# A vision tower on one core: scale folded into weights, small operations moved between engines, instruction lists in another order

## The chip, the cores and the metric

The kernel runs on one core of a Trainium2 chip. The time is the device time of one execution, in microseconds (us). The core has TensorE (matmuls, its weight loads shown as PEld), VectorE (DVE), ScalarE (ACT), GpSimd (POOL) and a queue engine (SP) that issues the DMAs. Each engine works off its own list of instructions in order; semaphores tie the lists together.

## The reference

The input x holds complex states, 64 time steps by 128 channels by 64 states by 2 (real, imaginary). The output is 64 x 129 x 1024. Per step (cut to what matters):

```python
h = s4d_kernel(log_dt, C=x, B, inv_A_real, A_imag, L=1024)      # (64, 128, 1024): sum over states of C * V**l
h = concatenate([broadcast(cls_tok), h], axis=1)                # (64, 129, 1024)
h = h + attn(layernorm(h))
h = h + ffn(layernorm(h))
# attn: down to 128, gelu, two hydra layers, gate, up to 1024
u = gelu(x @ w_down.T + b_down); xmid = u
u = hydra(hydra(u))
alpha = sigmoid(gate1)
out = x + (xmid + alpha * xmid + (1 - alpha) * u) @ w_up.T + b_up
# hydra: in-projection to z, xBC, dt; causal conv of 7 taps and silu; a forward and a backward
#   state-space scan over the 64 steps (4 heads of 64, 16 states); skip; times silu(z); rms norm; out-projection
# ffn: base linear 1024 -> 1024 + LoRA of 8 experts of rank 16, weighted by a router softmax over
#   15 logits of which the top 8 are kept
```

## The kernel before, in words

A tile is two of the 128 channels with their 64 steps each: 128 rows of 1024. There are 64 such tiles and one for the class token, 65 in all. The kernel is a software pipeline over iterations i = 0 to 69. In iteration i each engine works on up to five tiles at once: tile i (S4D kernel, first norm, down projection), tiles i-1 and i-2 (stages "H" and "G", the two halves of a hydra layer; the first layer of one tile and the second layer of the tile two behind it are done side by side), tile i-4 ("D": gate, up projection, second norm) and tile i-5 ("E": router, base linear, LoRA, store). All stages run in iterations 5 to 63. Iterations 8 to 61 are a hardware loop of two iterations per pass, the others are written out. On the way a tile's first norm result and u rest in DRAM (`carried`).

What each engine does in an iteration, and in which order, is an explicit list of calls at the end of its body: `grams()`, `turn_xs()`, ... for TensorE, `kernel_p()`, `gram(0)`, ... for VectorE, and so on. A step waits only for the semaphores named in it, and for what stands ahead of it in its engine's list. Large fp32 products are done as three fp32r matmuls with weights and activations split into a high and a low part (`w_hi`, `w_lo`, `XHI`, `XLO`); transposes and small products are plain fp32.

The steps that matter here:

- S4D (tile i): `turn_x` (TensorE) transposes the states into a PSUM bank; `keep_x` (ScalarE, L991) copies 256 columns to XTC, 128 real and 128 imaginary; `shift_real` (VectorE) and `shift_imag` (GpSimd) multiply them by three time shifts; `shift_none` (GpSimd, L831) copies the unshifted real part into W; `shift_sum` adds; `s4d(0)`, `s4d(1)` multiply; `keep_h` (ScalarE) copies the result to T; `stats_1` (VectorE), `root_1` (GpSimd), `shift_1` (VectorE, L1341: NM1 = -mean x root) and `norm_1` (ScalarE) make the normed H, which `turn_a` transposes and `down` projects. `deviation_1` and `carry_h` (GpSimd, L875) make h + norm(h) for the residual.
- Hydra: `grams`, `turn_xs`, `decay_sums` (TensorE), `gram`, `gram_forth`, `gram_sum`, `mix_matrix` (VectorE), `exp_decays` (ScalarE), `mix`, `skip` (GpSimd), `add_skip`, `times_z` (VectorE), `squares`, `norm_y` (ScalarE), `mean_square` (VectorE), `root_y` (GpSimd), `turn_y`, `keep_y`, `project_out`. `layer_out` (VectorE, L1282) copies the layer's output to U, the input of the next layer. `project_x`, `project_bc`, `project_z` project the next input; `conv` (VectorE, two halves by six taps) and `scale_bc` with `add_bc` (ScalarE and GpSimd, L895) convolve; `softplus(0..12)`, `split_decays`, `decays_forth`, `decays_back` make the decays for the next iteration; `silu_x`, `silu_bc` (L1066) end the convolution, and the next `grams` wait for them.
- Gate (tile i-4): `gated_a` (VectorE, L1348) scales xmid by 1 + alpha, `gated_b` (L1354) adds (1 - alpha) times the layer's output from PSUM; the sum is split (`gated_hi`, `gated_lo`) and multiplied in `up(0)`, `up(1)`. Then `residual`, `stats_2`, `root_2`, `shift_2` (VectorE, L1384), `norm_2`, `turn_d`, `split_hi`, `split_lo`.
- Router and FFN (tile i-5): `route(a, b)` and `bases(h, a, b)` are the blocks a to b-1 of 128 inputs of the router with LoRA-down (144 columns) and of half h of the base linear (512 columns), three matmuls per block. Router steps 0 to 8 (VectorE) with `exp_router`, `turn_h`, `keep_w` and `weighted_lo` (the split into HWS) lead to `lora(0)`, `lora(1)`, which close the banks; `final(0)`, `final(1)` add the residual, and SP stores.

The functions of one engine name lines that the profile shows under a helper: L929 is ScalarE's `copy`, L1512 the three matmuls of `ffn`.

Of the kernel before, what the change touches and what calls it, by code (L numbers as in the profile page):

```python
# [23 lines left out]
F32 = mybir.dt.float32  # L24
F32R = mybir.dt.float32r
I32 = mybir.dt.int32
ALU = mybir.AluOpType
# [3 lines left out]
P = 128  # L31
# [23 lines left out]
def build(nc, x, cls_tok, log_dt, tok_B, inv_A_real, A_imag, w_down, b_down, w_up, b_up, gate1, in_w,  # L55
# [19 lines left out]
    with ExitStack() as keep:  # L75
# [55 lines left out]
        with ExitStack() as tmp:  # L131
# [61 lines left out]
            s_albe, s_tab, s_vals, s_chain = tsem("s_albe"), tsem("s_tab"), tsem("s_vals"), tsem("s_chain")  # L193
            s_red, s_dec, s_sin, s_exp = tsem("s_red"), tsem("s_dec"), tsem("s_sin"), tsem("s_exp")
# [174 lines left out]
            def _(act):  # L369
# [87 lines left out]
            def _(dve):  # L457
# [115 lines left out]
                def second_parts(n):  # L573

                    for k, (src, m, dst, lo, _, _) in enumerate(jobs):
# [8 lines left out]
                        TT(lo, cols, dst.bitcast(F32), ALU.subtract).then_inc(s_lo, 1)  # L584

                for c in range(CHUNKS):
# [4 lines left out]
                    if c == 0:  # L591
# [5 lines left out]
                        link(TS(al1[:, :], al1[:, :], 1.0, None, ALU.add))  # L597
                second_parts(1000)
# [11 lines left out]
        XTC = sb("XTC", [P, 2, 2, CS])  # L610
# [60 lines left out]
        per = dict(cls_in=(1, 16), xswap=1, xt=1, xtc=1, wr=1, wi=2, wsum=1, v1=1, v2=1, vsum=1,  # L671
                   km=2, hev=4, st1=4, rs1=1, sd1=1, nm1=1, xh1=1, tt=1, tr1=2, xte=2, down=1, gelu=1,
                   pin=3, xms=1, conv0=4, conv=NCONV, cbm=TAPS - 1, cbc=TAPS - 1, dtc=NDT, asp=2, edt=1, xs=3, sz=1, trx=1, gram=1, xse=1,
# [61 lines left out]
        with nc.Block() as block:  # L735

            @block.sync
            def _(sp):
# [34 lines left out]
                def load_x(t, p):  # L773
                    wait(sp, t - 2, xt=1, xswap=1, v1=1, wr=1, v2=1, wi=2)
# [25 lines left out]
            def _(pool):  # L800
                def body(i, p):
# [21 lines left out]
                    def shift_imag():  # L823

                        if A:
                            wait(pool, i, xtc=1)
                            wait(pool, i - 1, wsum=1)
                            inc(pool.tensor_tensor(WI[:, :, :, :], XTC[:, 1, :, :].unsqueeze(2).broadcast_to([P, 2, 3, CS]),
                                                   TB[:, p, :, TSI].unsqueeze(3).broadcast_to([P, 2, 3, CS]), ALU.mult), "wi")

                    def shift_none():  # L831
                        if A:
                            wait(pool, i, xtc=1)
# [27 lines left out]
                    def root_1():  # L861
                        if A1:
                            wait(pool, i, st1=4)
                            wait(pool, i - 1, xh1=1, sd1=1)
                            inc(pool.tensor_tensor(RS1[:, :], VE1[:, :], half_neg[:, 0:1], ALU.pow), "rs1")  # L865

# [40 lines left out]
                    shift_none()  # L907
# [19 lines left out]
            def _(act):  # L927
# [3 lines left out]
                def body(i, p):  # L931
# [59 lines left out]
                    def keep_x():  # L991
                        if A:
                            wait(act, i, xt=1)
                            wait(act, i - 1, wr=1, wi=2)
                            copy(XTC[:, :, :, :].rearrange("p a b c -> p (a b c)"), bK[:, 0:256], "xtc")

# [33 lines left out]
                    def keep_y():  # L1030
                        if G:
                            wait(act, r, tyn=1, mm=1)
                            wait(act, r - 1, outp=1)
                            copy(YT[:, :, :].rearrange("p a b -> p (a b)"), bZ[:, :], "yte")

# [50 lines left out]
                    keep_x()  # L1086
                    keep_xs()
                    exp_decays()
# [8 lines left out]
                    keep_h(1, 0)  # L1097
                    keep_h(1, 1)
                    keep_y()
# [696 lines left out]
```

## Time and profile before

| | us |
|---|---|
| median of 3 runs | 2343.29 (2339.07 to 2344.38) |
| the profiled execution's own time | 2339.94 |
| its span, first to last instruction | 2338.2 |
| TensorE busy (weight loads) | 2161.3, 92% (1805.6, 77%) |
| VectorE busy | 1847.3, 79% |
| ScalarE busy | 1528.2, 65% |
| GpSimd busy | 1091.2, 47% |
| mean DMA rate | 57 GB/s |

The page cuts the span into 40 slices. TensorE is at 90% or more in the sixth and up to the last but one; its granted clock is in the top tenth from the sixth slice on. The first five slices or so are the set-up (weights transposed and split, tables) and the first iterations, in which few tiles are under way. Matmul durations are modelled and overlap, so it is the distance from start to start that counts. An engine's idle time on a line is followed by who ended it; "issue" means that nothing the profile shows was waited for.

### The profile page before, as it was taken

The numbers are of one execution on the slowest core, as the hardware profiler recorded it, in microseconds if no ns is written. First come the engines' busy times: TensorE is split into PE (matmuls) and PEld (weight loads), VectorE is DVE, ScalarE is ACT, GpSimd is POOL, SyncE is SP. The second block draws the span as 40 slices with busy tenths as digits, with TensorE's granted clock in tenths as the row PEclk, the third lists the DMA queues.
The fourth block names the chain that finished last, engine by engine and source line by source line (L and its number), as shares of the span: only waits on it lengthen the run. The fifth ranks groups of instructions, "written<-read, shape, count | busy, mean of one in ns | idle before, by whom it ended". The sixth has DMA issues, their size and how long they took to land.

```text
span 2338.2 us, 51899 instructions
## 1 busy us (share of the span) xinstructions
PE 2161.3 (92%) x14117; PEld 1805.6 (77%) x14117; DVE 1847.3 (79%) x4980; ACT 1528.2 (65%) x2921; POOL 1091.2 (47%) x1350
## 2 busy tenths in 40 slices
PE   1356799999999999999999999999999999999998
PEld 1245688888888888888888888888888888888776
DVE  6847688888888888888888888888888888888764
ACT  2546576766677766667666767666777666676652
POOL 2534355444455444455444554444554444554331
PEclk9756799999999999999999999999999999999999
DMA  4400122112222122221122221122211222211211
GB/s 92 117 29 24 35 64 64 42 54 63 63 63 61 35 61 63 63 63 48 47 63 63 63 63 40 55 63 63 63 58 36 63 63 63 63 47 47 69 39 33
DMA packets 90061, 132.61 MB, mean 57 GB/s; under 512 B 20379, under 2 KB 63559, under 8 KB 90006
## 3 DMA queue, kind: packets, MB, share of 16 engines
q1 hardware_dynamic: 79176, 125.60, 18.2%
q10 hardware_dynamic: 10830, 6.35, 1.1%
q8 instruction: 25, 0.41, 0.1%
q14 instruction: 30, 0.25, 0.0%
HBM read 55.17 MB, written 76.74 MB: 56 GB/s over the span
## 4 chain that ended last, share of the span: by engine, by line
issue 43%; PE 27%; POOL 9%; DVE 7%; ACT 6%; POOLq 1%; DVEq 0%; ACTq 0%; DMA 0%; SPq 0%
PE bank L1611 5%; PE bank L1512 5%; POOL CB L901 4%; PE bank L1567 3%; PE bank L1542 2%; DVE NF L1241 2%; ACT L1006 2%; POOL XD L852 2%; PE bank L1685 1%; PE bank L1669 1%; POOL RS L886 1%; PE bank L1544 1%; PE bank L1543 1%; POOL RS L865 1%; PE bank L1659 1%
## 5 line engine op out<-in xcount | busy, mean ns | idle before, releaser
L1512 PE MATMUL bank<-w_hi,XHI 128*128 128x512 f32 (+1 forms) x1560 | 622.9, 399 | 0.0
L1512 PE MATMUL bank<-w_lo,XHI 128*128 128x512 f32 (+1 forms) x1560 | 554.7, 356 | 0.0
L1512 PE MATMUL bank<-w_hi,XLO 128*128 128x512 f32 (+1 forms) x1560 | 554.4, 355 | 0.0
L1147 DVE SCALAR_TENSOR_TENSOR CX<-bank,cw,CX 128x252 f32<-128x252 f32 (+5 forms) x804 | 335.7, 460 | 61.8 <-ACT CX L944 61.6
L901 POOL TENSOR_TENSOR CB<-CB,CM 48x252 f32<-48x252 f32 (+5 forms) x402 | 292.7, 728 | 153.6 <-ACT CM L929 142.7
L1512 PEld LDWEIGHTS bank<-w_hi,XLO 128*128 128x128 f32 x1560 | 295.5, 189 | 46.9
L1512 PEld LDWEIGHTS bank<-w_lo,XHI 128*128 128x128 f32 x1560 | 296.8, 190 | 41.4
L1512 PEld LDWEIGHTS bank<-w_hi,XHI 128*128 128x128 f32 x1560 | 296.4, 190 | 41.2
L929 ACT ACTIVATE T<-bank 64x512 f32<-64x512 f32 x256 | 151.4, 592 | 261.1 <-PE bank L1601 256.5
L865 POOL TENSOR_TENSOR RS<-VE,half_neg 128x1 f32<-128x1 f32 x65 | 35.5, 546 | 369.9 <-DVE VE L1339 369.9
L892 POOL TENSOR_TENSOR RB<-m_gt,AS 128x512 fp32r<-128x512 f32 x134 | 164.9, 1231 | 56.8 <-DVE AS L1413 56.8
L929 ACT ACTIVATE CM<-CR,cwb 48x256 f32<-48x256 f32 x402 | 181.5, 497 | 3.7 <-POOL CB L901 1.5
L859 POOL TENSOR_TENSOR RS<-MS,half_neg 128x2 f32<-128x2 f32 x67 | 46.9, 700 | 242.8 <-DVE MS L1270 242.8
L1601 PE MATMUL bank<-VB,W 128*128 128x256 f32 x512 | 148.9, 415 | 7.4 <-DVE W L1212 5.2
L1395 DVE TENSOR_TENSOR XLO<-bank,XHI 128x512 fp32r<-128x512 f32 x130 | 89.9, 692 | 72.1 <-ACT XHI L929 72.1
L1401 DVE TENSOR_TENSOR RF<-m_lt,AS 128x512 fp32r<-128x512 f32 x134 | 142.9, 1105 | 0.0
L1611 PE MATMUL bank<-XHT,wdT 128*128 128x128 f32 x1040 | 135.8, 287 | 4.5 <-ACT XHT L929 4.5
L929 ACT ACTIVATE XHI<-bank 128x512 fp32r<-128x512 f32 x130 | 77.6, 597 | 94.7 <-PE bank L1567 94.7
L1611 PEld LDWEIGHTS bank<-XHT,wdT 128*128 128x128 f32 x1040 | 129.4, 203 | 6.1 <-ACT XHT L929 6.1
L844 POOL TENSOR_TENSOR NB<-GB,sp_dt 128x512 f32<-128x512 f32 x67 | 95.9, 1431 | 77.4 <-DVE GB L1224 77.4
L852 POOL TENSOR_TENSOR XD<-XS,DD 128x512 f32<-128x512 f32 x67 | 84.6, 1263 | 99.0 <-DVE DD L1232 54.2
L1601 PEld LDWEIGHTS bank<-VB,W 128*128 128x128 f32 x512 | 89.9, 196 | 23.1 <-issue 5.9
(295 smaller groups left out, 5332.5 us busy)
## 6 DMA issues: line engine op xcount, KB each, us to landing
carried<-T SPq DMA_DIRECT2D x65, 512.0 KB, 4.8
T<-carried SPq DMA_DIRECT2D x65, 512.0 KB, 3.9
out<-HB SPq DMA_DIRECT2D x129, 256.0 KB, 3.2
tables<-tab SPq DMA_DIRECT2D x8, 560.0 KB, 4.3
TB<-tables SPq DMA_DIRECT2D x64, 70.0 KB, 2.7
carried<-U SPq DMA_DIRECT2D x65, 64.0 KB, 3.6
XM<-carried SPq DMA_DIRECT2D x65, 64.0 KB, 4.8
XI<-in_x SPq DMA_DIRECT2D x128, 32.0 KB, 2.8
```

The source lines that it names most:

```text
L844: inc(pool.tensor_tensor(NB[:, :, :].rearrange("p (a h) t -> p a h t", a=2), GB[:, :, :].unsqueeze(2).broadcast_to([P, 2, NH, CS]), dtB, A ...
L852: inc(pool.tensor_tensor(XD[:, :, :], v3(XS[:, :], HD), DD[:, :].unsqueeze(2).broadcast_to([P, 2 * NH, HD]), ALU.mult), "xd")
L892: inc(pool.tensor_tensor(RB[:, part, :, :], m_gt[:, :].unsqueeze(1).broadcast_to([P, 2 * NH, CS]), decays(1, part), ALU.mult), "rb")
L901: inc(pool.tensor_tensor(CB[:, :, s:CS], CB[:, :, s:CS], CM[:, s % 3, :, 0:CS - s], ALU.add), "cbc")
L929: inc(act.activation(dst, src, ACT.Copy, scale=scale), name)
L1147: inc(STT(CX[:, c, :, s:CS], src[:, :, 0:CS - s], cw[:, c, k:k + 1], CX[:, c, :, s:CS], ALU.mult, ALU.add), "conv")
L1395: inc(TT(XLO[:, p, ks, :], v3(bT[:, :], P), XHI[:, p, ks, :].bitcast(F32), ALU.subtract), "xlo")
L1401: inc(TT(RF[:, part, :, :], m_lt[:, :].unsqueeze(1).broadcast_to([P, 2 * NH, CS]), decays(0, part), ALU.mult), "rf")
L1512: ins = mm(bank[:, 0:c1 - c0], xs_[:, 1 - p, k, :], ws[:, k, c0:c1], start=(c0 == HID and k == 0 and n == 0), stop=(last == k and n == 2))
L1567: ins = tr(bT[:, P * k:P * (k + 1)], T2[:, (4 * g + k) * P:(4 * g + k + 1) * P], ident[:, :])
L1601: ins = mm(bK[:, 256 * s:256 * (s + 1)], W[:, b, 2 * s:2 * s + 2, :].rearrange("p a c -> p (a c)"), VB[:, b, :, :].rearrange("p a c -> p ( ...
L1611: ins = mm(bK[:, 0:P], wdT[:, k, :], XHT[:, k, :], start=(k == 0), stop=(k == KC - 1))
```

## The change

- al1 = 1 + sigmoid(gate) is multiplied into the up projection's weights when they are transposed and split; be1 becomes (1 - alpha) / (1 + alpha). `gated_a` falls away, and GT = be1 x layer output + xmid.
- `shift_1` and `shift_2` go from VectorE to GpSimd, as a `tensor_scalar` of one column.
- `layer_out` goes from VectorE to ScalarE, where it also waits for `gated_b`, which reads the same bank.
- `keep_x` makes two copies of 128 columns: the real part goes into W's unshifted place, the imaginary part to XTC. `shift_none` falls away, and `shift_real` reads W.
- The lists of all four engines are put in another order.

The parts of the diff follow, in the order set-up, GpSimd, ScalarE; `shift_2` is `shift_1` with NM2, MV2, RS2.

```diff
-                        jobs.append((src, rows, hi, lo, 1.0, n))
+                        jobs.append((src, rows, hi, lo, al1[:, 0:1] if kind == "u" else 1.0, n))
...
+                    if n >= 0 and pieces[n][0] == "u":
+                        act.wait_ge(s_gate, 1)
...
-                        TT(lo, cols, dst.bitcast(F32), ALU.subtract).then_inc(s_lo, 1)
+                        if scale == 1.0:
+                            TT(lo, cols, dst.bitcast(F32), ALU.subtract).then_inc(s_lo, 1)
+                        else:
+                            STT(lo, cols, scale, dst.bitcast(F32), ALU.mult, ALU.subtract).then_inc(s_lo, 1)
...
+                        link(dve.reciprocal(gate[:, :], al1[:, :]))
+                        TT(be1[:, :], be1[:, :], gate[:, :], ALU.mult).then_inc(s_gate, 1)
...
-                    def shift_none():
-                        if A:
-                            wait(pool, i, xtc=1)
-                            wait(pool, i - 1, km=2)
-                            apart(pool)
-                            inc(pool.tensor_copy(W[:, :, 0, :], XTC[:, 0, :, :]), "wi")
+                    def shift_1():
+                        if A1:
+                            wait(pool, i, rs1=1)
+                            wait(pool, i - 1, xh1=1, tt=1)
+                            apart(pool)
+                            inc(pool.tensor_scalar(NM1[:, :], MV1[:, 0:1], RS1[:, 0:1], -1.0, ALU.mult, ALU.mult), "nm1")
...
                     gram_back()
                     shift_imag()
-                    shift_none()
                     skip()
                     root_y()
                     root_1()
                     add_bc(1)
-                    deviation_1()
                     add_bc(2)
+                    shift_1()
                     add_bc(3)
                     add_bc(4)
                     root_2()
+                    shift_2()
                     add_bc(5)
+                    deviation_1()
                     decays_back(0)
+                    carry_h()
                     add_bc(6)
                     decays_back(1)
-                    carry_h()
...
-                            copy(XTC[:, :, :, :].rearrange("p a b c -> p (a b c)"), bK[:, 0:256], "xtc")
+                            wait(act, i - 1, km=2)
+                            copy(W[:, :, 0, :], v3(bK[:, 0:P], CS), "xtc")
+                            copy(XTC[:, :, :], v3(bK[:, P:2 * P], CS), "xtc")
...
+                    def layer_out():
+                        if G:
+                            wait(act, r, outp=1)
+                            wait(act, r - 1, pin=3)
+                            if D:
+                                wait(act, td, gt=1)
+                            copy(U[:, p, 1, :], bY[:, 0:P], "u2")
...
                     keep_x()
+                    exp_decays()
                     keep_xs()
-                    exp_decays()
...
                     keep_h(1, 0)
+                    keep_y()
                     keep_h(1, 1)
-                    keep_y()
+                    layer_out()
                     exp_router()
...
-                    norm_1()
                     scale_bc(4)
                     scale_bc(5)
+                    norm_1()
+                    silu_z()
+                    keep_turned(0)
                     scale_bc(6)
-                    keep_turned(0)
-                    silu_z()
                     keep_w()
                     norm_2()
                     keep_turned(1)
+                    split_hi(0)
                     silu_x()
-                    split_hi(0)
                     silu_bc(0)
```

VectorE's list after the change, from the first tap to its end (the four moved or dropped steps are gone from it; ahead of the taps `kernel_p` now comes behind `gram(1)` and `kernel_sum` behind `shift_real`):

```
conv(1,0) conv(1,1) conv(2,0) conv(2,1) router(0) conv(3,0) router(1) stats_1(0) gated_b conv(3,1) stats_1(1)
router(2) router(3) router(4) gated_lo router(5) stats_1(2) conv(4,0) stats_1(3) conv(4,1) softplus(0) router(6)
softplus(1) residual(0) softplus(2) stats_2(0) softplus(3) router(7) conv(5,0) softplus(4) residual(1) softplus(5)
router(8) stats_2(1) softplus(6) conv(5,1) stats_2(2) softplus(7) stats_2(3) softplus(8) conv(6,0) softplus(9..11)
conv(6,1) softplus(12) weighted_lo split_decays(0) split_decays(1) decays_forth(0) split_lo(0) decays_forth(1)
final(0) split_lo(1) final(1)
```

TensorE's list before and after:

```
before: grams turn_xs decay_sums turn_x bases(0,0,1) route(0,1) bases(1,0,1) bases(1,1,2) route(1,2) bases(0,1,2)
 route(2,3) route(3,4) mix s4d(0) route(4,5) project_x route(5,6) s4d(1) route(6,7) route(7,8) bases(0,2,3)
 bases(0,3,4) turn_y bases(0,4,5) bases(1,2,3) project_out bases(0,5,6) project_bc up(0) bases(1,3,4) bases(0,6,7)
 up(1) project_z bases(1,4,5) turn_a(0) bases(0,7,8) bases(1,5,6) turn_h bases(1,6,7) turn_a(1) bases(1,7,8)
 lora(0) lora(1) turn_d(0) down turn_d(1)
after:  grams decay_sums turn_xs turn_x bases(1,0,1) route(0,1) bases(0,0,1) route(1,2) route(2,3) route(3,4)
 bases(0,1,2) mix route(4,5) s4d(0) route(5,6) bases(0,2,3) project_x s4d(1) bases(1,1,2) bases(1,2,3) route(6,7)
 turn_y route(7,8) bases(0,3,4) project_out bases(0,4,5) bases(0,5,6) project_bc up(0) project_z bases(1,3,4)
 up(1) bases(1,4,5) bases(1,5,6) turn_h bases(1,6,7) turn_a(0) bases(0,6,7) bases(1,7,8) turn_a(1) bases(0,7,8)
 lora(0) turn_d(0) down turn_d(1) lora(1)
```

## Rows read from the trace of the kernel before

**Rows 1.** Busy us of each engine in one stretch: start:end, length, engines, clock, DMA share, GB/s.
```profile
600.00:1200.00 600.00, 596.61 (x3967) 501.26 (x3964) 495.72 (x1374) 420.19 (x810) 292.40 (x355) 1.00 0.19 55
```

**Rows 2.** Waits of TensorE's weight loads, whole run: total us, times, longest.
```profile
PEld bank L1542 <- DVE HWS L1280: 33.5, 63, 1.2
PEld bank L1554 <- issue: 25.9, 64, 0.8
PEld bank L1636 <- issue: 22.3, 39, 1.4
```

**Rows 3.** TensorE in order of time, one iteration: start us, us, engine, line, operation.
```profile
1008.55 1.05 PE L1669 MATMUL bank<-fcT,CX 128*128 128x4 f32 x8
...
1017.30 1.13 PE L1601 MATMUL bank<-VB,W 128*128 128x256 f32 x4
...
1022.84 0.60 PE L1706 MATMUL bank<-ident,XD 128*128 128x128 f32 x4
...
1026.02 0.39 PE L1512 MATMUL bank<-w_hi,XLO 128*128 128x512 f32 x1
1026.46 0.61 PE L1636 MATMUL bank<-wbc,U 128*128 128x8 f32 x4
1027.01 0.63 PE L1638 MATMUL bank<-U,wbc 128*48 128x256 f32 x2
1027.57 0.51 PE L1554 MATMUL bank<-up_bias,row_sel 128*128 128x512 f32 x1
...
1035.82 0.40 PE L1512 MATMUL bank<-w_lo,XHI 128*128 128x512 f32 x1
1036.06 0.40 PE L1512 MATMUL bank<-w_hi,XLO 128*128 128x512 f32 x1
1036.53 0.50 PE L1542 MATMUL bank<-lb_hi,HWS 128*128 128x512 f32 x1
...
1040.69 0.95 PE L1669 MATMUL bank<-fcT,CX 128*128 128x4 f32 x8
```

**Rows 4.** VectorE in order of time, the same iteration.
```profile
1021.78 2.39 DVE L1147 SCALAR_TENSOR_TENSOR CX<-bank,cw,CX 128x252 f32<-128x252 f32 x6 [0.88 <-ACT CX L944]
...
1024.69 0.27 DVE L1352 TENSOR_SCALAR XM<-XM,al 128x128 f32<-128x128 f32 x1
...
1025.86 0.29 DVE L1286 COPY U<-bank 128x128 f32<-128x128 f32 x1
1026.07 0.34 DVE L1360 SCALAR_TENSOR_TENSOR GT<-bank,be,XM 128x128 f32<-128x128 f32 x1
...
1030.00 0.15 DVE L1346 SCALAR_TENSOR_TENSOR NM<-MV,RS 128x1 f32<-128x1 f32 x1
...
1035.19 0.64 DVE L1388 SCALAR_TENSOR_TENSOR NM<-MV,RS 128x1 f32<-128x1 f32 x1
...
1036.39 0.16 DVE L1413 TENSOR_TENSOR AS<-sp_aa,AS 128x16 fp32r<-128x16 f32 x1
```

**Rows 5.** ScalarE in order of time, the same iteration.
```profile
1011.85 0.39 ACT L929 ACTIVATE XTC<-bank 128x256 f32<-128x256 f32 x1 [0.84 <-PE bank L1620]
...
1021.71 0.91 ACT L972 ACTIVATE XD<-XD,RS 128x256 f32<-128x256 f32 x2
...
1039.58 0.42 ACT L1071 ACTIVATE CT<-CB 16x256 f32<-16x256 f32 x1
```

**Rows 6.** GpSimd in order of time, the same iteration.
```profile
1013.98 0.75 POOL L836 COPY W<-XTC 128x128 f32<-128x128 f32 x1
...
1029.13 0.73 POOL L901 TENSOR_TENSOR CB<-CB,CM 48x252 f32<-48x252 f32 x1 [1.27 <-ACT CM L929]
1029.83 0.22 POOL L873 TENSOR_SCALAR SD<-RS 128x1 f32<-128x1 f32 x1
...
1038.03 1.03 POOL L901 TENSOR_TENSOR CB<-CB,CM 48x232 f32<-48x232 f32 x1
...
1040.06 1.19 POOL L880 TENSOR_SCALAR T<-T,SD,NM 128x1024 f32<-128x1024 f32 x1
```

More of the change, by code:

```diff
@@ L573, in second_parts @@
                 def second_parts(n):
-                    for k, (src, m, dst, lo, _, _) in enumerate(jobs):
+                    for k, (src, m, dst, lo, scale, _) in enumerate(jobs):
                         if lo is None or k < nlo[0]:
@@ L609, in build @@
         XSW = sb("XSW", [P, NST, 2])
-        XTC = sb("XTC", [P, 2, 2, CS])
+        XTC = sb("XTC", [P, 2, CS])
         W = sb("W", [P, 2, 4, CS])
@@ L865, in root_1, with shift_2 @@
                             inc(pool.tensor_tensor(RS1[:, :], VE1[:, :], half_neg[:, 0:1], ALU.pow), "rs1")
+                    def shift_1():
[4 more added lines that the diff above has]
+                            inc(pool.tensor_scalar(NM1[:, :], MV1[:, 0:1], RS1[:, 0:1], -1.0, ALU.mult, ALU.mult), "nm1")
+                    def shift_2():
+                        if D:
+                            wait(pool, td, rs2=1)
+                            wait(pool, td - 1, xh2=1)
+                            apart(pool)
+                            inc(pool.tensor_scalar(NM2[:, :], MV2[:, 0:1], RS2[:, 0:1], -1.0, ALU.mult, ALU.mult), "nm2")
                     def deviation_1():
@@ L1377, in stats_2 @@
                             wait(dve, td, st2=2)
+                            wait(dve, td - 1, nm2=1)
                             apart(dve)
@@ L1382, in stats_2 @@
                             inc(TS(VE2[:, :], MV2[:, 1:2], EPS, None, ALU.add), "st2")
-                    def shift_2():
-                        if D:
-                            wait(dve, td, rs2=1)
-                            wait(dve, td - 1, xh2=1)
-                            inc(STT(NM2[:, :], MV2[:, 0:1], -1.0, RS2[:, 0:1], ALU.mult, ALU.mult), "nm2")
                     def split_lo(g):
@@ L1473, in body @@
                     softplus(7)
+                    stats_2(3)
                     softplus(8)
-                    router(8)
+                    conv(6, 0)
                     softplus(9)
@@ L1596, in s4d @@
                             if b == 0:
-                                wait(pe, i, xtc=1, wsum=1, wi=2, vsum=1)
+                                wait(pe, i, xtc=2, wsum=1, vsum=1)
                             else:
@@ L1719, in body @@
                     grams()
+                    decay_sums()
                     turn_xs()
-                    decay_sums()
                     turn_x()
+                    bases(1, 0, 1)
+                    route(0, 1)
                     bases(0, 0, 1)
-                    route(0, 1)
-                    bases(1, 0, 1)
-                    bases(1, 1, 2)
                     route(1, 2)
-                    bases(0, 1, 2)
                     route(2, 3)
                     route(3, 4)
+                    bases(0, 1, 2)
                     mix()
+                    route(4, 5)
                     s4d(0)
-                    route(4, 5)
+                    route(5, 6)
+                    bases(0, 2, 3)
                     project_x()
-                    route(5, 6)
                     s4d(1)
+                    bases(1, 1, 2)
+                    bases(1, 2, 3)
                     route(6, 7)
+                    turn_y()
                     route(7, 8)
-                    bases(0, 2, 3)
                     bases(0, 3, 4)
-                    turn_y()
+                    project_out()
                     bases(0, 4, 5)
-                    bases(1, 2, 3)
-                    project_out()
                     bases(0, 5, 6)
@@ L1757, in body @@
                     bases(1, 6, 7)
+                    turn_a(0)
+                    bases(0, 6, 7)
+                    bases(1, 7, 8)
                     turn_a(1)
-                    bases(1, 7, 8)
+                    bases(0, 7, 8)
                     lora(0)
-                    lora(1)
                     turn_d(0)
@@ L1764, in body @@
                     turn_d(1)
+                    lora(1)
                 UP, TURN_A, TURN_D = range(3)
```

84 lines of the change are left out of this document (32 added, 52 removed).

## The prediction, made before the result was known

> **What bounds the kernel now.** I read four views in this order. First the table by stretches: in the 600 us from 600 to 1200, TensorE's busy time is 596.6 us at a granted clock of 1.00, the 2.4 GHz level, while VectorE is busy 495.7, ScalarE 420.2 and GpSimd 292.4 [rows 1]. So in the steady part only two things can make the kernel faster: less TensorE work, or shorter holes between its matmuls. The diff leaves every matmul in place, in number and shape. What is left is holes. Second, who the weight loads waited for: over the whole run 33.5 us for the split of the weighted LoRA activations (L1280), 25.9 us at the first matmul of `up` (L1554) and 22.3 us at `project_bc` (L1636), these two as issue time [rows 2]. Those are idle times of the weight loader, and a matmul still runs beside part of them, so the loss has to be read from matmul starts.
>
> Third, the starts in one iteration, `grams` at 1008.55 to `grams` at 1040.69, 32.14 us [rows 3]. Neighbouring 512-column matmuls start 0.24 us apart where nothing waits (1035.82, 1036.06). At `project_bc` the step is 1026.46 − 1026.02 = 0.44, a hole of 0.20 us. From the 256-column matmuls at 1027.01 it is 0.56 us to `up(0)`, and I estimate 0.1 of that as a hole: L1554's 25.9 us over 65 iterations are 0.4 us of idle loader each, and the running matmuls cover most of it [rows 2]. At `lora(0)` the step is 1036.53 − 1036.06 = 0.47, a hole of 0.23. Together 0.53 us of 32.14. The fourth view, the other engines' instructions in order of time, says who is late there: VectorE writes U at 1025.86 and GT behind it at 1026.07, just before `project_bc`; and it runs without a gap from the first tap at 1021.78 to the second half of the decay split at 1036.39; the HWS split that `lora(0)` waits for comes directly ahead of that [rows 2, 4]. So VectorE's list between these points is the second limit, a fraction of a microsecond behind TensorE.
>
> **Part by part.** I count in microseconds after `grams`, t; a row at 1036.53 is t = 27.98.
>
> *VectorE loses four instructions.* The U copy (0.29 long, some 0.2 from its start to the next), the XM scaling (0.27; 0.18 to the next start), NM1 (0.15; 0.12) and NM2, whose row shows 0.64 for one column, 0.56 to the next start [rows 4]. That is 1.06 us out of the 14.75 us between the first tap and the end of the decay split. All lie on VectorE's gapless stretch. The new list puts back two waits I expect there: `router(0)` wants the last `route`, which TensorE now issues after `turn_y` (about 0.3 us idle), and the statistics want `keep_h(1,1)`, which ScalarE now does after `keep_y` (about 0.2). Net: the LoRA split ends 0.5 to 1.0 us earlier in t; I take 0.8, since the idle time replaces waits that the shorter list would have had anyway at the copies' place.
>
> *TensorE's order.* Summing the old starts' differences in the new order, with the holes taken out: `mix` arrives at about t 6.9, since a base block and a route that stood ahead of it now stand behind; `s4d(0)` (old t 8.75) at 8.5; `project_bc` (old 17.91) at 17.7; `up(0)` (old 19.02) at 18.7; `lora(0)` (old 27.98) at 27.5 [rows 3]. GT now needs only `project_out`, moved ahead of a base block, and ends at about t 16.8 against 17.9 before; the U copy follows it on ScalarE; its nearest row there is the XTC copy, 0.39 us for twice the columns, which I take as the upper end, with VectorE's 0.29 as the lower [rows 4, 5]. So U is there at 17.2, 0.5 before `project_bc`. Its hole goes, all but 0.05 us for the sequencer's waits: 0.15 saved. The hole at `lora(0)` goes whole, since HWS is ready 0.5 us ahead: 0.23 saved. The 0.1 at `up(0)` I leave: three waits are still put ahead of that matmul, and the view calls it issue time, not another engine [rows 2].
>
> *The U copy on ScalarE* waits for GT on purpose, and behind it stand the router's exponential, `gated_hi` and the first bias of the B/C convolution. In t these come at 17.1, 17.6 and after `project_bc` at 18.7; `gated_lo` then ends by 18.55 and `up(0)` wants it at 18.7. It is covered by 0.15 us only; if that is not so, each 0.1 us of delay is 6 us of kernel.
>
> *XTC as two copies, W's unshifted part in place.* Two instructions of 128 columns cost ScalarE at most 2 x 0.39 − 0.39 = 0.39 us more, at least 0.1. `exp_decays` now comes ahead of `keep_xs`, which takes more off its way than the second copy adds, so the exponential ends no later than before; `mix` wants XS by 6.9, and by the same sum has it at 6.3. GpSimd loses its copy of 0.75 us [rows 6] between the WI product and the skip product. The skip product waits for DD on VectorE, so this 0.75 is idle time there and worth 0, with 0.2 as its upper end. The DMA queue waits for `wi` at one count less; its transfers are two iterations ahead: 0.
>
> *The two shifts on GpSimd.* There is no row of that form. The nearest is the one-column SD instruction with 0.22 us; the upper end is the 0.75 that the 128-column copy took beside VectorE's products [rows 6]. I take 0.22 for each: 0.44 more, 0.75 less. NM1 then stands behind `add_bc(2)`, and `norm_1` behind `scale_bc(5)`; TensorE wants H at t 24.6 and has it at 23.1, so 0 either way. The same row of NM2 on VectorE, 0.64 us for one column where NM1 has 0.15, shows that the place it leaves is no cheap one [rows 4].
> The Trainium skill, "GPSIMD Engine Reference", section 4.1 "Engine selection", speaks against this move: elementwise work belongs on VectorE, and section 3.1 counts two software hops per instruction on GpSimd against one. The trace agrees in part: 0.22 us for SD against 0.15 for NM1, but not against NM2's 0.64. By the rule alone `shift_2` would make GpSimd's tail, the next item, later by the difference and C below likelier; by the rows the list is shorter than before, and I keep my chance for C.
>
> *GpSimd's tail.* This is the move that I distrust. Before, `decays_back(0)`, `add_bc(6)` (1.03) and `decays_back(1)` came ahead of `carry_h` (1.19 us) [rows 6]. Now `carry_h` is ahead of `add_bc(6)`, and `silu_bc` twice, and then `grams`, wait for that. In the old trace the second `silu_bc` starts at 1039.58 and takes 0.42, to t 31.45; `grams` starts at 32.14, a slack of 0.69 [rows 3, 5]. In the new order: slack 0.69, plus 0.8 (decays split earlier), minus 0.6 (TensorE earlier), minus 1.19, gives −0.30; `add_bc(6)` may go down from 1.03 towards 0.65 us (the same instruction with more columns, at 1029.13, took 0.73 [rows 6]; 0.65 is my estimate from it and 1.03 the other end), which gives +0.08 at best. So the hole is 0 to 0.3 us; I take 0.04, near the low end, because `lora(1)`, now last in TensorE's list, also covers the split of the second half, which follows on ScalarE.
>
> *Setup.* Two more one-column VectorE instructions and one wait on ScalarE: 0.4 us once, and the folded scale is read in copies that run anyway: 0.
>
> **Sum.** Per iteration −0.15 −0.23 +0.04 = −0.34 us. All stages run in iterations 5 to 63, 59 of them: −20. Setup +0.4. For the short iterations at both ends, where engines wait for each other's latency and not for TensorE, I take 0, with ±5. Against the profiled execution's 2339.94 (span 2338.2): 2320.3 us. Its own time lies 3.35 below the median of the three runs, 2343.29, and within their 5.3 us of spread, so the median may come as high as 2323. I say 2320.
>
> **The rivals.**
> *A: the full gain.* All holes close, those of `up(0)` too, and the tail opens none: −0.53 per iteration gives −31 us, and as much as −0.7 (−41) if the sequencer spends less on waits that are long fulfilled; about 2303. For it: VectorE's lead grows everywhere. Against it: two of the three entries in rows 2 are issue time, and the wait instructions stay.
> *B: the holes move.* The y chain (squares, mean, root, `norm_y`, ending at 1022.62) has 0.22 us before `turn_y` at 1022.84 [rows 3, 5]. `turn_y` arrives 0.45 earlier in t, while that chain follows `s4d(0)`, 0.27 earlier: 0.04 left. If ScalarE's added copies delay it by 0.4 us, the gain is used up: within 0.1 us an iteration, 2334 to 2344, about 2339. The Trainium skill, "TensorE: Matmul & The Clock Gate", section "Architectural detail: the array is 16x 32x32", says of the queue that only weight loads are pulled ahead, matmuls keep program order; so nothing behind `turn_y` would fill the hole, though ready bases stand there. By a queue that let them pass, B would cost nothing. The trace agrees with the rule: the hole at `lora(0)` stays open although ready matmuls follow.
> *C: slower, through GpSimd's tail.* If VectorE's split isn't earlier in t (the two new idle waits eat the 1.06 us), the slack is 0.69 − 0.6 − 1.19 = −1.10 against an iteration without holes, that is 1.10 − 0.53 = 0.57 us longer than now: +34 us, about 2374; with `add_bc(6)` shortened to 0.65, 0.19 longer: +11, 2351. It decides from the point where the split is less than some 0.5 us earlier. For it: 1.19 us is the largest single thing moved onto a path with 0.69 us of slack. Against it: NM2's 0.64 us alone gives that back.
>
> **How the numbers follow.** Forecast (2310 to 2330) 0.47; A 0.20; B 0.14; C 0.19. The range leaves out C's upper half and little of A: 2299 to 2350. The three runs differ by 0.2%, so less than that (4.7 us) can't be told from no change. Faster: the forecast, A and a third of B, 0.72; the rest of B and a little of C, 0.11 the same; slower 0.17.
>
> **What would show it.** Right: weight loads wait for HWS no longer, `lora(0)` starts 0.24 us behind the last base; `project_bc` names neither U nor GT; period 31.7 to 31.85 us; NM2's 0.64 is gone and each shift on GpSimd is near 0.22. B would show as waits of `turn_y` for XD from L972, or of `turn_h` for HW; C as weight loads of `grams` waiting for CT, and CT for CB. The prediction is wrong if the period stays at 32 us, or if the end iterations move by more than 5 us.

## The result, and the profile after

| | before | after |
|---|---|---|
| median, us | 2342.18 (4 runs, 2339.07 to 2344.38) | 2372.22 (4 runs, 2371.99 to 2374.03) |
| span of the profiled execution | 2338.2 | 2370.3 |
| start of the exponential (L1006, now L1025) in iterations 2, 8, 62, 68 | 172.2, 372.6, 2104.2, 2290.6 | 172.3, 366.4, 2136.4, 2320.6 |
| period, mean of iterations 8 to 62 | 32.07 | 32.78 |

The kernel became slower: the ratio is 1.0131, 95% interval 1.0113 to 1.0148. I had said 2320, faster. The third row shows where: the six iterations from 2 to 8 are 6.3 us shorter, the last six are 2.2 us shorter, and the 54 periods in between together 38.4 us longer, 0.71 each.

First the table by stretches, for the stretch of [rows 1]. TensorE, which had 596.6 us of 600, has 584.6: the holes grew.

```profile
600.00:1200.00 600.00, 584.64 (x3888) 492.38 (x3887) 493.60 (x1260) 412.08 (x827) 271.07 (x362) 1.00 0.19 56
```

Then the waits of TensorE's weight loads over the whole run, beside [rows 2].

```profile
PEld bank L1697 <- issue: 53.3, 67, 3.7
...
PEld bank L1554 <- DVE GTS L1303: 20.1, 37, 1.3
PEld bank L1685 <- DVE RF L1405: 17.3, 31, 0.6
PEld bank L1536 <- DVE HW L1341: 17.3, 63, 0.8
...
PEld bank L1706 <- ACT XD L989: 11.1, 8, 2.2
...
PEld bank L1636 <- issue: 3.0, 3, 1.3
...
PEld bank L1542 <- DVE HWS L1308: 1.9, 3, 0.7
```

HWS (L1308) costs 1.9 us where it cost 33.5: that hole closed as predicted. `project_bc` (L1636) has 3.0 of issue time instead of 22.3. New are `mix` (L1697, 53.3), `decay_sums` (L1685, waiting for RF, the product of VectorE's `decays_forth`), `up(0)` for GTS and `turn_h` for HW. So VectorE is late at all four places. Not all of it is one cause: in e1 below, where `decay_sums` waits no longer, the loads of `mix` still wait 34.0 us, those of `up(0)` 20.0 us for GTS and those of `turn_h` 16.6 us for HW. VectorE's instructions around the end of an iteration, in order of time:

```profile
1012.11 0.69 DVE L1405 TENSOR_TENSOR RF<-m_lt,AS 128x512 fp32r<-128x512 f32 x1
1014.41 0.69 DVE L1399 TENSOR_TENSOR XLO<-bank,XHI 128x512 fp32r<-128x512 f32 x1 [1.62 <-ACT XHI L946]
1015.02 3.23 DVE L1405 TENSOR_TENSOR RF<-m_lt,AS 128x512 fp32r<-128x512 f32 x1
1018.17 0.68 DVE L1423 TENSOR_TENSOR HB<-bank,HB 128x512 f32<-128x512 f32 x1
...
1019.97 0.27 DVE L1249 TENSOR_TENSOR GF<-bank,m_lt 128x126 f32<-128x126 f32 x1
...
1023.76 0.69 DVE L1282 TENSOR_TENSOR Mt<-NF,EX 128x512 f32<-128x512 f32 x1
```

The pair of RF products took 2.13 us together before. Now the first takes 0.69, and the second, behind `split_lo(0)` (XLO), 3.23 us, for 512 columns. It ends at 1018.25; HB, XLO, HB and the gram products line up behind it, GF starts at 1019.97, and `mix` waits for Mt. What GpSimd does meanwhile:

```profile
1010.73 0.28 POOL L881 TENSOR_SCALAR NM<-MV,RS 128x1 f32<-128x1 f32 x1 [0.20 <-POOL RS L902]
...
1012.27 1.42 POOL L908 TENSOR_TENSOR RB<-m_gt,AS 128x512 fp32r<-128x512 f32 x1 [0.45 <-DVE AS L1417]
1013.69 1.19 POOL L896 TENSOR_SCALAR T<-T,SD,NM 128x1024 f32<-128x1024 f32 x1
1014.85 0.59 POOL L917 TENSOR_TENSOR CB<-CB,CM 48x232 f32<-48x232 f32 x1
1015.40 1.04 POOL L908 TENSOR_TENSOR RB<-m_gt,AS 128x512 fp32r<-128x512 f32 x1
1016.39 0.28 POOL L821 COPY XSW<-XI 128x128 f32<-128x128 f32 x1
1016.65 1.05 POOL L828 TENSOR_TENSOR V<-TB 128x512 f32<-128x512 f32 x1
```

RB, T, CB, RB, XSW and V follow each other from 1012.27 to 1017.70 with no gap. VectorE's product was ready at 1015.02, during CB; it ends 0.55 us after V, somewhat less than the 0.69 of the first half, which nothing disturbs. It has been held through the rest of CB and three whole instructions. TensorE's starts around this (beside [rows 3]):

```profile
1012.22 0.39 PE L1512 MATMUL bank<-w_hi,XLO 128*128 128x512 f32 x1
1012.45 0.39 PE L1542 MATMUL bank<-lb_hi,HWS 128*128 128x512 f32 x1
...
1016.51 1.00 PE L1669 MATMUL bank<-fcT,CX 128*128 128x4 f32 x8
...
1018.38 0.50 PE L1685 MATMUL bank<-RF,earlier 128*128 128x256 f32 x2 [0.50 <-DVE RF L1405]
...
1024.60 1.15 PE L1697 MATMUL bank<-XS,Mt 64*64 64x64 f32 x32 [0.33 <-DVE Mt L1282]
...
1035.77 0.63 PE L1638 MATMUL bank<-U,wbc 128*48 128x256 f32 x2
1036.55 0.49 PE L1554 MATMUL bank<-up_bias,row_sel 128*128 128x512 f32 x1
```

and the next `grams`:
```profile
1049.28 1.00 PE L1669 MATMUL bank<-fcT,CX 128*128 128x4 f32 x8
```

`grams` to `grams` is 32.77 us. `lora(0)` follows the last base by 0.23: no hole. `decay_sums` finds TensorE 0.5 us idle, `mix` 0.33, and `up(0)` comes 0.78 after the 256-column matmuls, where it was 0.56.

### The profile page after: what moved, and what is told of

The parts are those of the page before. It is cut to its first block, busy times and chain, and to the rows that moved or that the text cites. A ratio compares the mean times of both kernels' runs of the same rounds, so it can differ in the third digit from the quotient of the medians.

```text
span 2370.3 us, 51893 instructions
## 1 busy us (share of the span) xinstructions
PE 2153.7 (91%) x14117; PEld 1804.3 (76%) x14117; DVE 1860.8 (79%) x4720; ACT 1536.9 (65%) x3052; POOL 1043.4 (44%) x1416
## 4 chain that ended last, share of the span: by engine, by line
PE 61%; DVE 22%; issue 7%; ACT 3%; DVEq 1%; POOL 1%; DMA 0%; ACTq 0%; SPq 0%; POOLq 0%
PE bank L1512 25%; PE bank L1601 5%; DVE NF L1269 4%; PE bank L1697 3%; DVE NF L1275 3%; PE bank L1611 3%; PE bank L1716 2%; PE bank L1578 2%; DVE RF L1405 2%; PE bank L1627 2%; PE bank L1645 2%; DVE HB L1423 2%; PE bank L1554 2%; PE bank L1567 2%; DVE Mt L1282 2%
## 5 line engine op out<-in xcount | busy, mean ns | idle before, releaser
L1175 DVE SCALAR_TENSOR_TENSOR CX<-bank,cw,CX 128x252 f32<-128x252 f32 (+5 forms) x804 | 351.6, 461 | 62.5 <-ACT CX L961 62.5
L917 POOL TENSOR_TENSOR CB<-CB,CM 48x252 f32<-48x252 f32 (+5 forms) x402 | 263.6, 656 | 55.4 <-ACT CM L946 32.2
L1405 DVE TENSOR_TENSOR RF<-m_lt,AS 128x512 fp32r<-128x512 f32 x134 | 244.5, 1827 | 0.0
L946 ACT ACTIVATE CM<-CR,cwb 48x256 f32<-48x256 f32 x402 | 188.5, 500 | 11.2 <-POOL CB L917 6.1
L853 POOL TENSOR_TENSOR XD<-XS,DD 128x512 f32<-128x512 f32 x67 | 77.1, 1151 | 173.3 <-DVE DD L1260 94.1
L1601 PE MATMUL bank<-VB,W 128*128 128x256 f32 x512 | 143.1, 404 | 7.9 <-DVE W L1240 5.4
L1601 PEld LDWEIGHTS bank<-VB,W 128*128 128x128 f32 x512 | 95.1, 197 | 24.6 <-issue 6.0
```

Of the source, the lines that this page charges most:

```text
L853: inc(pool.tensor_tensor(XD[:, :, :], v3(XS[:, :], HD), DD[:, :].unsqueeze(2).broadcast_to([P, 2 * NH, HD]), ALU.mult), "xd")
L917: inc(pool.tensor_tensor(CB[:, :, s:CS], CB[:, :, s:CS], CM[:, s % 3, :, 0:CS - s], ALU.add), "cbc")
L946: inc(act.activation(dst, src, ACT.Copy, scale=scale), name)
L1175: inc(STT(CX[:, c, :, s:CS], src[:, :, 0:CS - s], cw[:, c, k:k + 1], CX[:, c, :, s:CS], ALU.mult, ALU.add), "conv")
L1405: inc(TT(RF[:, part, :, :], m_lt[:, :].unsqueeze(1).broadcast_to([P, 2 * NH, CS]), decays(0, part), ALU.mult), "rf")
L1601: ins = mm(bK[:, 256 * s:256 * (s + 1)], W[:, b, 2 * s:2 * s + 2, :].rearrange("p a c -> p (a c)"), VB[:, b, :, :].rearrange("p a c -> p ( ...
```

## The experiments

The theory after the two traces: VectorE's second RF product, moved behind `split_lo(0)`, falls into an unbroken run of GpSimd and is starved of something the two share. The rivals: my case C (`carry_h` ahead of `add_bc(6)`), and TensorE's new order (`decay_sums` ahead of `turn_xs`). Times are medians; ratios are to the kernel before in the same job, with 95% intervals. Periods are the means from iteration 8 to 62.

**The product moved back (e1).**
```diff
                     decays_forth(0)
+                    decays_forth(1)
                     split_lo(0)
-                    decays_forth(1)
                     final(0)
```


> The changed kernel with one call moved back in VectorE's list: the second half of decays_forth stands again ahead of split_lo(0). Starvation theory: in the changed kernel this product with two SBUF operands starts at 1015.02 just as GpSimd begins an unbroken run of five instructions, ends 3.2 us later, at 1018.25, and makes decay_sums, the gram step, mix and up(0) late; moved back it runs beside one decays_back, takes no more than 1.5 us, and the period falls from 32.78 to 31.7-31.9 us, the time to 2310-2325 us. Tail theory (my case C: carry_h ahead of add_bc(6) delays silu_bc and grams): nothing changes, about 2372. Order theory (decay_sums now ahead of turn_xs): half of the hole, about 0.5 us, stays, 2340-2372.


Measured: 2326.83 us, ratio 0.9944 (0.9926 to 0.9962), period 31.95. One call in its old place takes 45 us off and makes the kernel faster than before; by the expectations on record neither rival alone does that. The time is 2 us above the stated range, and the reason is in this kernel's instructions in order of time, TensorE's, ScalarE's and GpSimd's:

```profile
1030.68 1.05 PE L1669 MATMUL bank<-fcT,CX 128*128 128x4 f32 x8 [0.20 <-ACT CT L1098]
```

ScalarE:
```profile
1030.13 0.42 ACT L1098 ACTIVATE CT<-CB 16x256 f32<-16x256 f32 x1
```

GpSimd:
```profile
1027.49 1.62 POOL L896 TENSOR_SCALAR T<-T,SD,NM 128x1024 f32<-128x1024 f32 x1
1029.08 0.58 POOL L917 TENSOR_TENSOR CB<-CB,CM 48x232 f32<-48x232 f32 x1
```

`carry_h` (T) takes 1.62 us instead of 1.19, held by the second RF, which ends at 1028.04. CB, that is `add_bc(6)`, ends at 1029.66, so the second `silu_bc` (CT) ends at 1030.55 and TensorE stands idle for 0.20 us before `grams`. That is C's mechanism, really there, but not what made the changed kernel slow.

**`turn_xs` first again (e2).**
```diff
                     grams()
-                    decay_sums()
                     turn_xs()
+                    decay_sums()
```


> The changed kernel with turn_xs ahead of decay_sums in TensorE's list again, VectorE's list as changed. Order theory: the hole of 0.5 us ahead of decay_sums is the loss, and the time falls by 30 us to 2340. Starvation theory: VectorE still ends its product at the same place and the lateness reaches the gram step and mix; the hole only moves to mix, the period falls by 0.1 us at most, 2366-2374 us. Tail theory: no change.


Measured: 2374.17 us, ratio 1.0143 (1.0121 to 1.0165), period 32.76. The hole only moves, as the theory said, though first to the next tile's first base matmul and not to `mix` (L1530, idle for 0.30 us at 1019.25 until VectorE's HB); TensorE's order is not the cause.

**A gap in GpSimd's run (e3).**
```diff
                             wait(pool, q, asp=2)
                             wait(pool, r, seg=1)
+                            if part == 1:
+                                wait(pool, q, rf=2)
```


> The changed kernel with one wait added on GpSimd: the second half of decays_back waits until VectorE has done both halves of decays_forth. Starvation theory: the wait opens a gap after add_bc(6) at about 1015.4, in which VectorE's product gets through (about 0.7 us from there, its row about 1.1 us long instead of 3.2); RB comes 0.7 us later, still before decay_sums, and the time falls although a wait was added, to 2310-2330 us. Tail theory and order theory: an added wait makes nothing faster, 2372 or more.


Measured: 2301.53 us, ratio 0.983 (0.9813 to 0.9848), period 31.51: 71 us off the changed kernel by adding a wait, and 8 us below my range. VectorE, then GpSimd:

```profile
1021.48 0.86 DVE L1407 TENSOR_TENSOR RF<-m_lt,AS 128x512 fp32r<-128x512 f32 x1
```

GpSimd:
```profile
1020.04 1.18 POOL L896 TENSOR_SCALAR T<-T,SD,NM 128x1024 f32<-128x1024 f32 x1
1021.19 0.59 POOL L919 TENSOR_TENSOR CB<-CB,CM 48x232 f32<-48x232 f32 x1
1022.50 1.04 POOL L910 TENSOR_TENSOR RB<-m_gt,AS 128x512 fp32r<-128x512 f32 x1 [0.72 <-DVE RF L1407]
```

GpSimd idles 0.72 us after CB, RF gets in as soon as CB is done and takes 0.86 us in the place where it took 3.23. Since `carry_h` has nothing of VectorE's beside it here (1.18 us), the wait of `grams` is gone as well; that is part of the 71 us.

**The same move in the kernel before (e4).**
```diff
                     decays_forth(0)
-                    decays_forth(1)
                     split_lo(0)
+                    decays_forth(1)
                     final(0)
```


> The kernel before with one call moved in VectorE's list: the second half of decays_forth behind split_lo(0), as the change does. Starvation theory: there GpSimd's list runs unbroken until 1042.5 (carry_h is last of it), so the product that starts at about 1040.0 ends at about 1043.1, gram is late by over 2 us, of which mix has 0.8 us of slack: the period rises by 1 to 1.8 us, 2400-2450 us. Tail theory and order theory: within 0.2 us of the period, at most 2350.


Measured: 2439.2 us, ratio 1.0428 (1.041 to 1.0447), period 33.76. The one call alone, in a kernel that has none of the other edits, costs 97 us. RF is held until V is through:

```profile
1009.50 2.60 DVE L1401 TENSOR_TENSOR RF<-m_lt,AS 128x512 fp32r<-128x512 f32 x1
```

GpSimd:
```profile
1010.49 1.05 POOL L820 TENSOR_TENSOR V<-TB 128x512 f32<-128x512 f32 x1
```

**The product back and GpSimd's old tail (e5).** The kernel of e1 with
```diff
                     decays_back(0)
-                    carry_h()
                     add_bc(6)
                     decays_back(1)
+                    carry_h()
```


> The run e1_rf_back with GpSimd's tail in the order of before as well: add_bc(6) and decays_back(1) ahead of carry_h. In e1 the loads of grams still wait up to 0.7 us, matmuls 0.2 us, for the second silu_bc, and the period is 31.88 us against 31.43 in e3. Tail theory, now as a second and smaller cause behind the starved product: the wait goes, the period falls to 31.4-31.5, the time to 2298-2308 us. If the rest of e1 over e3 is something else, about 2327 us.


Measured: 2299.99 us, ratio 0.9822 (0.9806 to 0.9838), period 31.47. (The expectation's 31.88 and 31.43 for e1 and e3 are 31.95 and 31.51 by the means used here.) In this kernel TensorE is as full as it gets in any run here:

```profile
600.00:1200.00 600.00, 598.23 (x4056) 511.01 (x4057) 487.80 (x1320) 428.20 (x861) 288.44 (x382) 1.00 0.20 58
```

**The edits alone, in the old lists (e6).** `gated_a`, `shift_none` and VectorE's three moved steps are taken out of the old lists and `layer_out`, `shift_1` and `shift_2` put in on their new engines.


> Only the edits, with all four lists as before (the moved steps put in at the nearest old place: layer_out behind keep_y, shift_1 behind add_bc(1), shift_2 behind root_2). VectorE's list is about 1 us shorter, so the hole of 0.23 us ahead of lora(0) closes; U now comes behind GT, on ScalarE, so the 0.20 us ahead of project_bc stay. The two halves of decays_forth stand together, nothing is starved: period 31.8-31.9, 2326-2334 us. If the edits themselves are harmful, over 2342 us.


Measured: 2333.84 us, ratio 0.9976 (0.9966 to 0.9986), period 31.94. The edits are good for some 7 us; the new orders, with the two calls put back as in e5, for another 34. The U copy on ScalarE, behind GT, leaves a hole ahead of `project_bc` (start, duration, and the idle time before it with its releaser); one of 0.20 us was expected, and this is more:

```profile
1022.52 0.61 PE L1636 MATMUL bank<-wbc,U 128*128 128x8 f32 x4 [0.36 <-ACT U L946]
```

**GpSimd's old tail alone (e7).** The changed kernel with the tail edit shown above and nothing else.


> The changed kernel with nothing but GpSimd's tail in the order of before. My case C (carry_h ahead of add_bc(6) is what made the kernel slower): 2340 us or less. Starvation theory: GpSimd's run of instructions is as long and as unbroken in this order, VectorE's product that starts at about 1015.0 still takes about 3 us, and the time stays at 2365-2376 us.


Measured: 2374.7 us, ratio 1.0147 (1.013 to 1.0164), period 32.78, the same as the changed kernel's. RF comes while GpSimd's second RB is running, takes 3.21 us and ends 0.55 after V (VectorE, then GpSimd):

```profile
1013.40 3.21 DVE L1405 TENSOR_TENSOR RF<-m_lt,AS 128x512 fp32r<-128x512 f32 x1
```

GpSimd:
```profile
1012.59 1.03 POOL L908 TENSOR_TENSOR RB<-m_gt,AS 128x512 fp32r<-128x512 f32 x1
...
1015.01 1.05 POOL L828 TENSOR_TENSOR V<-TB 128x512 f32<-128x512 f32 x1
```

Case C is refuted as the cause.

**One operand instead of two (e8).** The changed kernel; the mask is left out of the second half:
```diff
+                            if part == 1:
+                                inc(dve.tensor_copy(RF[:, part, :, :], decays(0, part)), "rf")
+                            else:
```


> The changed kernel, all lists as changed, but the second half of decays_forth is a copy with one SBUF operand; the mask is left out of that half. If VectorE is held only where it reads two SBUF operands while GpSimd's instructions follow each other, the copy takes 0.6-0.7 us in the same place and the time falls to 2300-2315 us. If any VectorE instruction on SBUF is held there, or the loss has another cause, it stays at 3 us and 2372 us. Either way it starts at the same place, just ahead of GpSimd's add_bc(6).


Measured: 2356.55 us, ratio 1.007 (1.0053 to 1.0086), period 32.49. Of the branch "any VectorE instruction" the 3 us came true, the 2372 us did not: the copy is held, and the time fell by 16 us all the same. The copy ends 0.29 us after V where the product ended 0.55 after it, and the period is 0.29 us shorter. Up to V's end it is held like the product:

```profile
1011.29 2.96 DVE L1406 CAST RF<-AS 128x512 fp32r<-128x512 f32 x1
```

GpSimd:
```profile
1012.91 1.05 POOL L828 TENSOR_TENSOR V<-TB 128x512 f32<-128x512 f32 x1
```

So two tensor operands are not the condition. Nor is it every VectorE instruction on SBUF. In e6 a BATCH_NORM_STATS2 of 512 columns that reads SBUF alone and starts 0.17 us after a CB takes 0.68 us; held to the end of that CB it would have taken 1.0, an estimate from CB's usual 0.63 us and the 0.55 after it. In e1 the HB sum, which has one operand in PSUM, takes 0.68 beside T (VectorE of e6, GpSimd of it, VectorE of e1):

```profile
1026.47 0.68 DVE L1384 BATCH_NORM_STATS2 ST<-HB 128x6 f32<-128x512 f32 x1
```

GpSimd, e6:
```profile
1026.30 1.37 POOL L917 TENSOR_TENSOR CB<-CB,CM 48x248 f32<-48x248 f32 x2
```

VectorE, e1:
```profile
1028.92 0.68 DVE L1423 TENSOR_TENSOR HB<-bank,HB 128x512 f32<-128x512 f32 x1
```

The Trainium skill, "SBUF — State Buffer", section "SBUF: two separate sides", has the rule that fits: VectorE in a two-port mode, or with two SBUF inputs against a GpSimd instruction that reads SBUF, and GpSimd take one port pair as a lock, each for a whole instruction. It also says that an fp32 copy from SBUF to SBUF runs in such a mode, so by it the copy, too, is held; the traces agree. The Trainium skill says there that who starts first gets the pair; it doesn't say who gets it next.

**Another instruction between the halves, in the kernel before (e9).**
```diff
-                    conv(6, 1)
                     ...
                     decays_forth(0)
+                    conv(6, 1)
                     decays_forth(1)
```


> The kernel before with conv(6,1), which reads PSUM, moved between the two halves of decays_forth. There the second half comes while GpSimd's decays_back(0) is in its place, and that one had itself waited for VectorE (1.42 us instead of 1.04). Question: what lets a VectorE product in between two GpSimd instructions. If it gets in when the GpSimd instruction in progress had waited for VectorE (taking turns once both wait), the second half still takes 1.5 us at most and the time stays at 2335-2348 us. If it gets in only when it directly follows another two-operand VectorE instruction, it is held until GpSimd's run ends 4 us later and the time rises above 2420 us.


Measured: 2326.81 us, ratio 0.9949 (0.9929 to 0.9968), period 31.85. VectorE, then GpSimd:

```profile
1001.66 1.16 DVE L1401 TENSOR_TENSOR RF<-m_lt,AS 128x512 fp32r<-128x512 f32 x1
```

GpSimd:
```profile
1000.85 1.43 POOL L892 TENSOR_TENSOR RB<-m_gt,AS 128x512 fp32r<-128x512 f32 x1 [0.49 <-DVE AS L1413]
1002.23 1.04 POOL L901 TENSOR_TENSOR CB<-CB,CM 48x232 f32<-48x232 f32 x1
```

RB had waited for the first RF (1.43 us instead of 1.04), and the second RF got in as soon as RB was done, at 1002.28; then CB waited in turn (1.04 instead of 0.59). It is not adjacency that lets VectorE in. Beside e7 this is the closest pair that the runs have: in both, RF comes 0.81 us after the start of a 512-column RB with the next GpSimd instruction right behind. Here RB had waited and RF gets in after it; there RB had not (1.03 us), and RF is held to the end of the run. The next instruction differs, though (CB here, T there). The time is a surprise, 8 us under the range: the LoRA split comes one tap earlier, the loader's wait for HWS is down to 0.2 us an iteration, and the period is 0.21 us shorter, about the 0.23 us of the hole at `lora(0)`.

**Both halves late (e10).** The changed kernel with `decays_forth(0)` behind `split_lo(0)` too.


> The changed kernel with both halves of decays_forth behind split_lo(0). The first of them now comes at the place where the second was starved, while add_bc(6) runs on GpSimd without having waited. By taking turns only once both wait, it is held to the end of GpSimd's run, 3.2 us, and the second follows in 0.6: decay_sums is 0.6 us later than in the changed kernel, 2395-2415 us. If a pair of such instructions next to each other is let in, the first takes 1.1-1.5 us and the time falls below 2350 us.


Measured: 2416.99 us (2 runs), ratio 1.0331 (1.0271 to 1.0391), period 33.53, 2 us over the range. The profiled run had a mean granted clock of 0.97 from 600 to 1200 us, where the others had 1.00, so its surplus is not all the product's.

```profile
1001.96 3.34 DVE L1405 TENSOR_TENSOR RF<-m_lt,AS 128x512 fp32r<-128x512 f32 x2
```

The first half comes while RB is running, is held through it, XSW and V (which ends at 1004.15), and the second follows: 3.34 us for both. A pair next to each other isn't let in either.

**What the traces hold besides.** From 400 us on, every 512-column product of VectorE with both operands in SBUF that GpSimd holds at all, in all twelve traces, goes by one pattern where GpSimd's next instruction follows without a gap: if the GpSimd instruction in progress had itself waited for VectorE, the product is let in behind it, otherwise it is held to the end of GpSimd's run. Smaller products break the pattern. In the changed kernel, e1, e2, e3, e5, e7, e8 and e10, a 16-column product (0.17 us where nothing holds it, L1212 in the changed kernel) comes during a CB that had not waited, and gets in at that CB's end although SD follows without a gap (VectorE, then GpSimd):

```profile
1011.26 0.43 DVE L1212 TENSOR_TENSOR sp_aa<-sp_dt,negA 128x16 f32<-128x16 f32 x1
```

GpSimd:
```profile
1010.97 0.69 POOL L917 TENSOR_TENSOR CB<-CB,CM 48x236 f32<-48x236 f32 x1
1011.64 0.18 POOL L889 TENSOR_SCALAR SD<-RS 128x1 f32<-128x1 f32 x1
```

The product ends at 1011.69, before SD does. (The 236-column CB takes 0.67 us at the least in any trace, so it wasn't held.) Whether it is the size of the product or the one-column SD behind that makes the difference, no run here tells. Nor is it always VectorE that is held: in three of the last iterations of e6, as at 2212.24, a CB takes 1.89 us instead of 0.69, and both halves of RF pass ahead of it.

## Why the prediction was wrong

Point by point, by its own steps.

*What bounds the kernel.* Right. TensorE was the bound, with 0.53 us of holes; the version with the two orders put back has a period of 31.47, 0.59 less than before.

*VectorE loses four instructions.* Right. The HWS wait fell from 33.5 to 1.9 us.

*The step that failed: the end of VectorE's list.* The prediction summed VectorE's list up to "the end of the decay split" and priced nothing behind it, though the new list shows the second half of `decays_forth` behind `split_lo(0)`. A moved step was costed at nothing and no cover was named for it. What the runs showed: the same instruction takes 1.53 us in its old place and 3.2 us in its new one; undoing it in the changed kernel gives −45 us (e1), doing it in the old one gives +97 us (e4), and opening GpSimd's run gives −71 us (e3, the tail's share included). The old trace had the sign: its second RF took 1.53 us of the pair's 2.13, its NF product beside NB 1.53, `shift_none` 0.75 beside VectorE and 0.28 alone. I used the last of these only as an upper bound for GpSimd.

*GpSimd's tail.* I gave its hole as 0 to 0.3 us and took 0.04. With RF back in its place it costs 0.47 us per iteration, 27 us in all (e1 with 31.95 against e5 with 31.47), and `carry_h` is itself held for 0.43 us of that; where nothing holds it (e3) the period is 31.51, 0.04 above e5's, which is the size I took. With RF late the tail costs nothing (e7). The mechanism of case C exists. Its number, 2374, is within 2 us of the measured one, by accident: as the cause it is refuted.

*The sum.* From before to e5 −0.59, the tail +0.47 (e5 to e1), the late product +0.83 (e1 to after): together +0.71 us per iteration, the measured change. The shares depend on the order in which they are taken: with the old tail the late product alone costs 1.30 (e5 to e7). The gain that I predicted at 0.34 is 0.59, near the size of rival A, but A's mechanism, which closes the hole at `up(0)` too, is not what did it, as the next point shows.

*`up(0)` and the U copy on ScalarE.* The copy takes 0.28 us, 0.01 under my lower end. But the 0.15 us by which I had `gated_lo` (GTS) covered are not there. In e5, TensorE's starts and the waits of its loads:

```profile
1008.35 0.63 PE L1638 MATMUL bank<-U,wbc 128*48 128x256 f32 x2
1009.12 0.50 PE L1554 MATMUL bank<-up_bias,row_sel 128*128 128x512 f32 x1
```

```profile
PEld bank L1554 <- DVE GTS L1303: 20.2, 38, 1.3
...
PEld bank L1554 <- issue: 16.2, 27, 0.6
```

The step is 0.77 us instead of 0.56, and the loads wait 36.4 us over the run instead of 25.9. So 0.21 us an iteration, some 12 us, stood in my sum at nothing. More than that came back where I had counted nothing: besides its hole, `project_bc` takes 0.44 us to the next start instead of 0.55, and the two S4D groups (L1601), counted the same way, 1.40 together instead of 1.57. In the old lists the U copy leaves a hole at `project_bc` instead (e6). *The shifts on GpSimd* take 0.28 (NM2, in the rows of GpSimd above), my 0.22 was close.

*The short iterations.* I took 0 with ±5. The first ones gained 8.7 us up to iteration 6 (136.7 to 128.1 us from iteration 2), outside that.

*Rival B* did not occur: the loads of `turn_y` wait 11.1 us over the run, in 8 iterations, against 12.0 in 13 before. `turn_h` waits for HW as B would show, 17.3 us of the loader, yet 31.47 us is reached in e5 with 16.5 us of that wait in place. The sign that I gave for B's queue rule, ready matmuls behind the hole at `lora(0)`, does not hold for what stands directly behind it: `lora(1)` wants the same HWS, and `turn_d` a T that ScalarE writes from 1035.94 to 1037.18, past the 1036.53 at which `lora(0)` starts.

## What to carry to other kernels

An order of instructions is not only a matter of semaphores. When you move a long VectorE instruction that works from SBUF to SBUF, look at what GpSimd does at its new place: with a gap there it costs little more than its own time, in an unbroken run it can cost the rest of the run. A wait put into GpSimd's list at the right place can be worth more than the work saved (71 us in e3, some 7 for all the edits).

## What the runs showed of the hardware

- A VectorE product of 512 columns, SBUF to SBUF, that comes while a GpSimd instruction is running which itself had not waited, is held through all GpSimd instructions that follow without a gap: 3.23, 3.21 and 2.60 us instead of 0.69, ending 0.55 us after GpSimd's last.
- If the GpSimd instruction in progress had waited for VectorE, the two take turns (RF 1.16 us in e9, and the pair of 2.13 us in the kernel before). This pattern fits every held 512-column product from 400 us on in the twelve traces (for RF: turns in the kernel before, e1, e5, e6 and e9; held in the changed one, e2, e4, e7, e8 and e10), but it is read from them, and 16-column products do not follow it (0.43 us, let in at the end of a CB that had not waited). A run that changes only whether the GpSimd instruction had waited was not made, and why it should be so stays open.
- A 512-column copy that ends 0.29 us after GpSimd's last is held like a two-operand product (2.96 us). Statistics on one SBUF operand and sums with a PSUM operand are not (0.68 us beside GpSimd's work).
